# Cross-attention and a routed feed-forward on one core: a new order behind the attention, exponentials on GpSimd, 18 row buffers, three levels of tiles, and the last two tiles summed on chip

## The reference, cut to what matters

```python
# x, ctx: (16, 128, 128); 16 tiles of 128 tokens, model width 128
x = x + xattn(layernorm(x), ctx, ctx)      # per token: 16 heads of width 8 against 16 heads of ctx
x = x + ffn(layernorm(x))

def ffn(inputs, router_w, wv, sv, w, s, w1, s1):      # E = 8 experts, K = 2 of them per token, F = 512
    x = inputs.reshape(B * S, Dm)                     # 2048 tokens
    probs = softmax(x @ router_w)
    expert_gate, expert_index = top_k(probs, K)
    xb = repeat(x, K, axis=0)                         # 4096 pairs of token and expert
    v = selected_matmul(xb, wv, sv)                   # 128 -> 512 by the pair's expert
    y = gelu(selected_matmul(xb, w, s))               # 128 -> 512
    out = selected_matmul(v * y, w1, s1)              # 512 -> 128
    return sum over k of expert_gate * out
```

## Time and profile before

| | |
|---|---|
| Time, median of three runs (lowest, highest) | 255.67 us (251.92, 257.34) |
| Profiled execution | 256.52 us, with a span of 254.7 us from its first to its last instruction |
| TensorE busy | 222.4 us (87% of the span) |
| VectorE, GpSimd, ScalarE busy | 182.1 us, 144.6 us, 130.9 us |
| Chain that ended last, by engine | TensorE 64%, VectorE 18%, issue 6%, DMA 4%, ScalarE 4%, GpSimd 2% |
| Mean granted TensorE clock | 0.957 of full speed |

### The profile page before, as it was taken

The page is one execution under the profiler, slowest core; times in us unless marked ns, Lnnn a source line. Parts: engine busy times, 40 slices in busy tenths (PEclk is TensorE's granted clock), DMA queues, the critical chain, the costliest instruction groups (busy, mean ns, idle before and its releaser), DMA issues.

```text
span 254.7 us, 6311 instructions
## 1 busy us (share of the span) xinstructions
PE 222.4 (87%) x1825; PEld 213.2 (84%) x1826; DVE 182.1 (71%) x436; ACT 130.9 (51%) x362; POOL 144.6 (57%) x158
## 2 busy tenths in 40 slices
PE   7997999997999788957977969999999999999900
PEld 6995988997989688856977969999999999999900
DVE  2699799899899988997356865656656646566471
ACT  2415646668766864736584523645545545455200
POOL 6956646654598689878673454443453535343330
PEclk9999999999999999995799988999999999999985
DMA  4979999999200000012312011122121212000853
GB/s 119 305 147 414 346 319 390 381 378 380 73 23 13 21 31 23 21 42 61 71 52 55 21 35 52 55 64 64 43 65 51 75 55 59 32 18 6 242 155 99
DMA packets 25518, 30.93 MB, mean 121 GB/s; under 512 B 2652, under 2 KB 16896, under 8 KB 25362
## 3 DMA queue, kind: packets, MB, share of 16 engines
q1 hardware_dynamic: 19852, 24.36, 30.7%
q0 software_dynamic: 2528, 4.77, 5.8%
q10 hardware_dynamic: 3110, 1.47, 2.0%
HBM read 16.26 MB, written 14.79 MB: 122 GB/s over the span
## 4 chain that ended last, share of the span: by engine, by line
PE 64%; DVE 18%; issue 6%; DMA 4%; ACT 4%; POOL 2%; DVEq 1%; another core or an unknown queue 1%; POOLq 0%; ACTq 0%; SPq 0%
PE bank L1078 26%; PE bank L1097 12%; PE bank L949 7%; PE bank L996 6%; DVE qk L1221 4%; PE bank L883 3%; DVE pv L336 3%; DMA expert_out<-yo,xs 3%; PE bank L1004 2%; PE bank L1062 2%; ACT w_sb L704 1%; DMA pv<-expert_out 1%; PE bank L958 1%; PE bank L927 1%; PE bank L1007 1%
## 5 line engine op out<-in xcount | busy, mean ns | idle before, releaser
L622 POOL DMA_INDIRECT expert_out<-yo,xs x39 | 40.5, 1039 | 53.7 <-DMA expert_out<-yo,xs 28.2
L336 POOL TENSOR_TENSOR pv<-probs,ctx_sb 128x1408 f32<-128x1408 f32 x14 | 40.1, 2867 | 21.1 <-DVE probs L1272 21.1
L1078 PE MATMUL bank<-xsT,g_tile 128*128 128x128 f32 x312 | 42.7, 281 | 5.4 <-ACT xsT L806 3.1
L580 POOL DMA_INDIRECT routed<-rows,pos x32 | 36.5, 1141 | 17.5 <-DMA routed<-rows,pos 8.0
L1078 PEld LDWEIGHTS bank<-xsT,g_tile 128*128 128x128 f32 x312 | 38.9, 196 | 6.3 <-issue 4.0
L1097 PE MATMUL bank<-w_sb,hid 128*128 x312 | 42.2, 279 | 0.0
L1078 PE MATMUL bank<-xsT,v_tile 128*128 128x128 f32 x312 | 42.2, 279 | 0.0
L1429 DVE TENSOR_TENSOR hid<-bank,act_sb 128x512 f32<-128x512 f32 x39 | 26.9, 690 | 19.2 <-PE bank L1078 13.1
L1420 DVE TENSOR_TENSOR g_tile<-g_sb,g_scale 128x512 f32 x39 | 26.9, 693 | 17.1 <-issue 12.3
L1097 PEld LDWEIGHTS bank<-w_sb,hid 128*128 128x128 f32 x312 | 38.8, 196 | 0.2 <-issue 0.2
L1078 PEld LDWEIGHTS bank<-xsT,v_tile 128*128 128x128 f32 x312 | 38.9, 196 | 0.0
(11 more groups left out here) (191 smaller groups left out, 313.1 us busy)
## 6 DMA issues: line engine op xcount, KB each, us to landing
routed<-pad_rows SPq DMA_DIRECT2D x4, 2080.0 KB, 20.1
xs<-routed SPq DMA_DIRECT2D x39, 65.0 KB
g_sb<-in_L_ffn_w_dram SPq DMA_DIRECT2D x1, 2048.0 KB, 11.1
g_scale<-in_L_ffn_s_dram SPq DMA_DIRECT2D x1, 2048.0 KB, 15.7
v_sb<-in_L_ffn_wv_dram SPq DMA_DIRECT2D x1, 2048.0 KB, 26.5
pv<-expert_out SPq DMA_DIRECT2D x3, 512.0 KB, 5.3
x_sb<-in_x_dram SPq DMA_DIRECT2D x4, 256.0 KB, 6.2
ctx_sb<-in_ctx_dram SPq DMA_DIRECT2D x4, 256.0 KB, 6.2
```

Source lines behind the costliest of these rows:

```text
L336: return eng.tensor_tensor(pv[:, b, g0:g1, :, :], probs[:, b, :, g0:g1].rearrange("p h g -> p g h").unsqueeze(3).to_broadcast([P, many, H, ...
L580: pool.indirect_dma_start(out=routed[:, :], out_offset=bass.IndirectOffsetOnAxis(ap=pos[:, m % TOP, m // TOP:m // TOP + 1], axis=0), in_=r ...
L622: pool.indirect_dma_start(out=expert_out[:, :], out_offset=bass.IndirectOffsetOnAxis(ap=xs_i[:, t % XB, P:P + 1], axis=0), in_=yo[:, t % X ...
L1078: mm = nc.tensor.matmul(psum[:, n * P:n * P + P], weights[:, c % 2, n * P:n * P + P], xsT[:, c % 2, :], start=True, stop=True)
```

## The change

Its parts, which come in one diff:

- **Order.** TensorE, ScalarE and VectorE get a new order from the last two attention tiles to tile 6. Each step now has a turn, the products and a down product from tile 0 on, the fourth group's second layer norm (`normed`, `turned`, `rows_but_gates`) stands behind the first tiles, its choices are cut in `maxima` and `ranked`, and the last table's pieces (`late_ends` to `late_rows`) stand one each behind steps 6 to 11 (tiles 7 to 12) instead of between tiles 2 and 4. TensorE gets 9 filler products (`keep_warm`) behind the output of attention tile 14.
- **GpSimd's power.** For the fourth group the exponential of the logits is `euler ** r2` on GpSimd, 128x40 elements, and ScalarE's two table loads and its exponential go.
- **GpSimd's order.** The third group's scatters begin before `second_rstd` of the fourth, go in pairs between its parts, and wait for the pair before to have landed.
- **Buffers.** XB is 18. The loop of 12 tiles becomes one of 18; VectorE's is written out.
- **Three levels.** Tiles 0 to 30 hold all rows of token tiles 0 to 11, tiles up to 34 those of token tiles 12 and 13, the last four those of 14 and 15. SyncE gathers three chunks when 31 tiles have landed, the fourth when 35 have, the fifth when 37 have.
- **On chip.** Tiles 37 and 38 are not scattered. GpSimd builds a matrix of ones and zeros for each (`owners`, behind the scatter of tile 32), and TensorE multiplies them with `yo` into a bank that already holds the residual. Their rows in `expert_out` are cleared early by a DMA.
- **Sums.** VectorE adds the first three chunks behind tiles 33 to 37 (`FINAL`), GpSimd adds the pairs of the last two chunks.

```diff
-DONE_T = NT - 2
-COVER = (TOP * TOKENS * DONE_T // NT + E * (P - 1)) // P
+DONE = (NT - 4, NT - 2, NT)
+COVER = [(TOP * TOKENS * t // NT + E * (P - 1)) // P for t in DONE[:-1]]
+KEPT = 2
+SENT = TILES - KEPT
-XB = 12
+XB = 18
...
+        def pairs_of(eng, n, done):
+            two, part, _ = pair_of(n)
+            eng.wait_ge(got_rows[n], 16)
+            eng.tensor_tensor(part, two[:, :, 0, :], two[:, :, 1, :], ALU.add).then_inc(done, 1)
...
-                for end, chunks in ((COVER, range(len(CHUNKS) - 1)), (TILES, range(len(CHUNKS) - 1, len(CHUNKS)))):
+                for level, end in enumerate((*COVER, SENT)):
                     for b in range(XB):
                         sp.wait_ge(y_sent[b], 16 * len(range(b, end, XB)))
...
-                        if n >= MID_G and m and m % 2 == 0:
+                        if n >= EARLY_G and m and m % 2 == 0:
...
+                def last_exponentials():
+                    pool.wait_ge(euler_set, 1)
+                    pool.wait_ge(logits_shifted, NG)
+                    pool.tensor_tensor(r3[:, :, :], euler[:, :, :], r2[:, :, :], ALU.pow).then_inc(logits_exp, 1)
...
-                for t in range(TILES):
+                for t in range(SENT):
...
+                    if t == COVER[0] + 1:
+                        for n in range(KEPT):
+                            owners(n)
+                for n in range(3, len(CHUNKS)):
+                    pairs_of(pool, n, pool_sum)
...
+                for n in range(KEPT):
+                    pe.wait_ge(whose_ready, n + 1)
+                    pe.wait_ge(yo_ready, SENT + n + 1)
+                    for m in range(LAST):
+                        mm = nc.tensor.matmul(bank[7][:, m * P:m * P + P], whose[:, n, m * P:m * P + P], yo[:, (SENT + n) % XB, :],
+                                              start=False, stop=(n == KEPT - 1 and m == LAST - 1))
...
+                FINAL = {33: (lambda: add_pairs(0),), 34: (lambda: add_rows(0),), 35: (lambda: add_pairs(1),),
+                         36: (lambda: add_rows(1), lambda: add_pairs(2)), 37: (lambda: add_rows(2),)}
```

More of the change, by code:

```diff
@@ L12 @@
+import math
 from contextlib import ExitStack
@@ L165, in xattn_moe_kernel @@
         r3 = sb("r3", [P, G, E + TOP])
+        euler = sb("euler", [P, G, E + TOP])
         pick = sb("pick", [P, TOP, G, E])
@@ L346, in xattn_moe_kernel, with ffn_steps @@
         assert TILES - 3 == full * XB
-        def ffn_steps(eng, ffn, first):
+        def ffn_steps(eng, ffn, first, between=None, late=None):
             for k in range(first, XB):
                 ffn(0, k)
-            with eng.Fori(1, full) as i:
-                for k in range(XB):
-                    ffn(i, k)
-            for k in range(2):
-                ffn(full, k)
+                if between and k in between:
+                    between[k]()
+            if full - bool(late) > 1:
+                with eng.Fori(1, full - bool(late)) as i:
+                    for k in range(XB):
+                        ffn(i, k)
+            for t in range((full - 1) * XB if late else full * XB, full * XB + 2):
+                ffn(t // XB, t % XB)
+                for piece in (late or {}).get(1 + t, ()):
+                    piece()
         def y_bank(t, c):
@@ L454, in _ @@
                 whole = TILES // XB
-                for c in range(MID, 2 * XB):
+                for c in range(MID, whole * XB if whole <= 2 else 2 * XB):
                     load(c // XB, c % XB)
-                with sp.Fori(2, whole) as i:
-                    for c in range(XB):
-                        load(i, c)
+                if whole > 2:
+                    with sp.Fori(2, whole) as i:
+                        for c in range(XB):
+                            load(i, c)
                 for c in range(TILES - whole * XB):
@@ L795, in value_weights @@
                         act.wait_ge(mid_ready, 1)
-                    if not isinstance(t, int) and c == MID - XB:
+                    if isinstance(t, int) and t == MID:
                         act.wait_ge(table_ready, 1)
@@ L1390, in late_tiles @@
[L1390 to L1391 removed]
+                                          bank[7][:, 128:128 + LEVELS * E].unsqueeze(2).to_broadcast([P, LEVELS * E, NT]),
+                                          tile_edges[:, :, :].unsqueeze(1).to_broadcast([P, LEVELS, E, NT]), ALU.is_gt))
+                    table(v.tensor_reduce(ends[:, :, :], over2[:, :, :, :], AX_X, ALU.add))
@@ L1398, in late_experts, with late_offsets @@
                     table(v.tensor_reduce(laps[:, :], passed2[:, :, :], AX_X, ALU.add))
-                    table(v.scalar_tensor_tensor(tile_e[:, late], passed2[:, :, E - 1], -float(E), laps[:, :], ALU.mult, ALU.add))
+                    for a in range(1, LEVELS):
+                        table(v.scalar_tensor_tensor(tile_e[:, late], passed2[:, :, a * E - 1], -float(E),
+                                                     laps[:, :] if a == 1 else tile_e[:, late], ALU.mult, ALU.add))
+                def late_offsets():
+                    table(v.tensor_tensor(jumps2[:, :, :], passed2[:, :, :],
+                                          flat(jump2[:, :, :]).unsqueeze(1).to_broadcast([P, LEFT, LEVELS * E]), ALU.mult))
```

228 lines of the change are left out of this document (139 added, 89 removed).

## The result

The changed kernel takes 263.99 us (median of 4 runs, 261.62 to 265.1), the kernel before 256.13 us beside it: ratio 1.039, 95% interval 1.020 to 1.058. It is slower, by 2 to 4%; the forecast said level (254.0 us for the profiled execution, 253.1 for the median). Executions of one kernel on one chip differ by up to 3%, and a ratio compares the faster ones of each kernel alone, so it need not be the ratio of the medians. The profiled execution took 263.17 us, its span 261.4 us, where I had forecast 252.2.

What follows compares the result with a forecast made beforehand. GpSimd's late scatters were taken to bound the end: first chunk at 231.9 plus 20.3 us gave a span of 252.2, plus 1.8 a time of 254.0, less 0.85 a median of 253.1 us; range 245.5 to 258.5.

Steps and rivals of the forecast that it cites:

- The chain from GpSimd's scatters to the first chunk: VectorE behind tile 33 waits 9 us for the first gathered chunk: tile 30's scatter at 224.6, chunk at 231.9.
- The order before the tiles: Attention's end: first product at 118.3 instead of 121.57; third group's scatter pairs from 116.7, the last issued at 133.3.
- The power: Fourth group's 128x40 exponential on GpSimd: 6.4 us by a line through three widths, from 133.4 to 139.8.
- cheap power: Rival: the 40-column power takes 1.0 us, fourth group's scatters start 2.2 us earlier, 250.9 us; chance 0.22.
- The hole of TensorE: Gate weights of tile 7 wait behind `positions` for the power, so TensorE idles about 2.4 us.
- shared port rival: GpSimd's power holds up VectorE's two-input products: 1.3 us later, 254.4 us; a variant within the main case's 0.50.
- Eight scatters: Fourth group's scatters on GpSimd: 16.2 us with usual 2.1 us landings, from 141.8 to tile 0's scatter at 158.0.
- The pace: GpSimd's scatters from tile 0 to tile 30: 2.22 us each, thirty of them, tile 30's at 224.6.
- the point (227.1): Start of tile 30's scatter at which the expensive chunk decides: 254.7 less the 27.6 us from it to the end.
- The step list from there to the store: From the first chunk's arrival: tile 36's scatter issued after 10.3 us, store finished after 20.3 us.
- The rival with the expensive chunk: Same wait at `add_pairs(0)` with cadence 2.30 and a gather of 5.3 us: time 256.7 us; chance 0.13.
- 18 buffers: XB = 18 row buffers never wait, which 12 would have done; costs nothing and gives nothing more.

Runs made afterwards that it cites:

- e13: Changed kernel with each tile scatter from tile 2 on waiting for the landing of the one two back: 258.98 us, ratio 1.006 to the kernel before.
- e10: e6 with the kept tiles' masks (`owners`) written behind the last scatter: 256.52 us, ratio 0.992 to the kernel before.
- e1: Changed kernel with the pair sums of the last two chunks on VectorE again: 259.73 us, ratio 1.010 to the kernel before.
- e2: Kernel before plus a one-column write on GpSimd after the last gathered chunk: 263.6 us against 259.35 for the kernel before, no ratio given.
- e4: Changed kernel with VectorE's sums of the first three chunks behind all tiles again: 261.46 us, ratio 1.021 to the kernel before.
- e6: Changed kernel with last group's exponentials on ScalarE, last two pair sums on VectorE, first three chunks' sums behind all tiles: 253.28 us, ratio 0.983 to the kernel before.
- e12: e6 with 12 row buffers in place of 18, tiles from 12 on in a loop again: 257.14 us, ratio 0.997 to the kernel before.
- e8: Changed kernel with up to four scatters under way, last exponentials on ScalarE and last two pair sums on VectorE: 259.01 us, ratio 1.009 to the kernel before.
- e9: Kernel before with an odd tile's scatter waiting for the landing of the one three back: 264.33 us, no ratio given.
- e11: e6 with each tile scatter from tile 2 on waiting for the landing of the one two back: 253.77 us, ratio 0.987 to the kernel before.
- e16: e11 repeated: 254.44 us, ratio 0.980 to the kernel before.
- e7: Changed kernel with an odd tile's scatter waiting for the landing three tiles back, up to four under way: 267.96 us, ratio 1.040 to the kernel before.

## Why the forecast was wrong

Two steps failed: the pace of the scatters was sized too low, and the end was put at the store's landing, where GpSimd's queue ends later. The chain from GpSimd's scatters to the first chunk was the right one (e13); the sizes in it, nearly all on the same side, and the missing term made 252.2 us into 261.4.

- **The order before the tiles**: right. First product at 118.02 (forecast 118.3), at full clock. The third group's four pairs at 115.75, 120.53, 125.34 and 131.08 (116.7, 121.7, 126.4 and 130.9), the last record's end at 133.89 (133.3).
- **The power**: the line through three widths gave 6.4 us, measured 6.82; cheap power is refuted. With a hand-over from `positions` of 1.9 us as forecast, the group's first scatter came at 142.71 (141.8). The hole of TensorE was 3.85 us (2.4). The two-input product of VectorE at 136.18 ran in 0.69 us under the power, as without it, so the shared port rival falls too.
- **Eight scatters**: 17.4 us, not 16.2. I had taken short landings because the loads of tile rows would be through. They were not: the last of eight was issued at 143.7, and GpSimd stood 3.05 and 2.60 us for the first two pairs' landings, 2.10 for the third's. Tile 0's scatter at 160.14, +2.1 us with the above.
- **The pace**: of the terms that stood in the sum this one failed most. I took 2.22 us, between an undisturbed pair and the mean of 2.30 in the earlier trace rows, for no reason that a row gave. It was 2.33; the mean stood in the rows, and the kernel before needs 2.32 from tile 0 to tile 30 ((222.58 - 153.05) / 30), though there the last three follow the results. Thirty scatters make +3.3 us, so tile 30's came at 230.07, 3 us beyond the point (227.1) which I had named as that from which the kernel is slower. From there to the first chunk it took 6.5 us, 0.8 less than forecast. The chunk was there at 236.6 instead of 231.9.
- **The step list from there to the store** held: scatter of tile 36 9.9 us after the chunk (10.3), store landed after 20.7 us (20.3). `owners` took 5.5 us (3), nearly free in its place: the landing of tile 32's scatter, at 239.8 beside the gathers, would have held GpSimd almost as long (e10).
- **The missing term**: the end of GpSimd's queue. By moving the last pair sum to GpSimd the change moved GpSimd's last instruction from 246.9 to 254.8 and with it the queue's end from 1 us ahead of the store's to 3.9 us behind. The row was there in the trace of before (8.80 us from 244.7), and I had not looked at the closing instructions. e1, e2 and e4 show it.
- **Range and chances**: +2.1 + 3.3 - 0.8 + 0.4 + 3.9 = 8.9 of the 9.2 us. The rival with the expensive chunk (256.7, chance 0.13) came nearest, for its cadence of 2.30; its gather of 5.3 us did not come (3.9). With it and the queue's end the median would have been 260.6, against 263.99.
- **18 buffers**: that they never wait, where 12 would, was right; "gives nothing more" was loose. Without them e6 loses 3.9 us (e12).

What the runs add: taking back the power gives 4.1 us, taking back the last sums 4.3 us, and both with the third part 10 to 11 us, which leaves a kernel 2% under the one before: 253 to 254 us. Loosening the pace alone gives 5 us (e13). How the order, the three levels and the kept tiles share this gain was not taken apart; of the buffers e12 tells.

## What to carry to other kernels

When work goes to an engine that is late, count every landing it waits for at the mean of its own rows; an idle share of 40% that is all landings is no reserve. Read each engine's closing instructions too: an engine whose queue takes long to end must have its last work early, however small that work is. And before loosening a wait that looks like caution, look at what the other engines do while it is loose.

## What the runs showed of the hardware

**GpSimd's queue ends 6.3 to 6.7 us after its last instruction**, in all 18 traces, whatever that is: a scatter (before 6.6, e6 6.4), a 0.7 us sum (6.4 in the changed kernel and in e13), a memset of one column (6.6), a 0.6 us subtraction (6.4 in e10). The other engines' closings took 0.01 to 0.8 us (TensorE's 1.3 in e10). The Trainium skill, Perfetto Trace Analysis, section "DMA Instruction — SWDGE (GPSIMD)", says that the profiled window of a GpSimd DMA ends with its descriptors and leaves the movement out; the trace agrees (0.97 us recorded, 2.3 us to landing), but that does not explain the queue's end, which is the same behind a memset.

**A row of GpSimd's scatters without a pause stops TensorE, VectorE and ScalarE**: in e8 TensorE for 2.8 and then 4.8 us and VectorE for 4.1 and 6.6, beside twelve at 1.27 us, in e9 TensorE for 2.5 us beside six, in e11 and e16 VectorE and ScalarE for 0.7 to 3.1 us at a time with at most two under way, and hardly where every second scatter waited for the one ahead to land. Over 140 to 200 us the waits on "remote" sum to 26.6 us in e8, 5.4 in e7, 11.1 in e9, 9.1 in e11, 18.1 in e16 and 8.7 in e13, and to none in the changed kernel. The Trainium skill, SBUF — State Buffer, section "SBUF: two separate sides", tells of GpSimd being kept from writing descriptors by VectorE; what stands here is the other side, and with it TensorE and ScalarE, engines that by that page don't share that port. Whether it is semaphores or instructions that reach them late was not tried and stays open. From 158 to 175 us the trace of e8 has no packet in the two instruction queues (q8 and q14), where the changed kernel's has three; but the next one in e8 comes at 178, 5 us after the engines went on.

**A power on GpSimd costs 0.16 us a column**: 1.01 us at four, 6.82 at forty, (6.82 - 1.01) / 36.

**A scatter beside large gathers lands late.** Beside the three gathers of 512 KB the scatter issued at 230.43 in e10 landed after 5.3 us, and those at 233.06 and 234.34 in the changed kernel after 5.2 and 5.5 us, against 2.3 us in the median from 160 to 225 us.
